# VectorE's order at the end of each head pair, the first step's order on ScalarE and GpSimd, and a third bank for the first products

## The chip, the cores and the metric

One core of one Trainium2 chip runs the whole program in one launch. The metric is the device time of that launch in microseconds, as a median of several runs. On a core, TensorE multiplies matrices, VectorE and ScalarE work on rows of vectors, GpSimd works on vectors and SyncE starts the DMAs. The program writes each engine's instructions in one list; an engine takes its list in order and waits on semaphores that the others count up.

## The reference

The input is layer-normalised, goes through lightning attention with a decay per head (16 heads of 128, blocks of 64 tokens in the reference, of 128 in the kernel), is RMS-normalised and gated, projected back, and multiplied by the SiLU of a router's mixture. Cut to what matters here:

```python
x = L0_attn_hidden_states                  # (4, 512, 512): 4 sequences of 512
xn = layernorm(x)
qkv = silu(xn @ w_qkv.T)                   # q, k, v of 16 heads
def step(kv, blk):
    o_inter = (q * q_decay) @ kv
    o_intra = ((q @ k.T) * diag_decay) @ v
    kv_new = block_decay * kv + (k * k_decay).T @ v
    return kv_new, o_inter + o_intra
out = norm_w * (out * rsqrt(mean(out * out) + eps))
s = (sigmoid(xn @ w_gate.T) * out) @ w_out.T
flat = xn.reshape(B * S, H)
scores = softmax(flat @ router_weight.T + router_bias)
topk_w, topk_idx = top_k(scores, 8)
g = silu(flat * sum(topk_w) + einsum(topk_w, expert_bias[topk_idx]))
return x + s * g
```

## The kernel before

The weights come in eight pairs of heads, the tokens in two halves (two sequences of 512 each). A half is a run over the eight pairs, so there are 16 steps, numbered `ss` 0 to 15; step 0 is the prologue, written out by hand, and `step(...)` on each engine writes steps 1 to 15. Step 8 (`close`) also finishes the output of the first half, step 15 (`final`) is the last; steps 6 and 14 carry the router's columns too.

Every matrix is split into a high and a low part in fp32r and a product is three matmuls. The products of queries and keys (groups `QK0` and `QK1`, one per head of the pair) and of the gates (`GATE`) go by seven block products (`p1`, `p2`, `p6`, `p5`, `p7`, `p4`, `p3` in this order) in place of eight; between them VectorE takes the partial sums out of the banks `st_ps` (`e1` to `e7`), ScalarE applies SiLU or tanh (`act_c11`, `act_c22`, `act_c21`, `act_c12`). Step 0 uses plain products (`direct_block(j)`, j 0 to 11), with the transposes of the tokens (`fill`) among them, banks `st_ps[0]` and `st_ps[1]` in turn.

A head h and a sequence b of a step make a unit (h, b), and for each there are, in this order: `turn_and_score` on TensorE (keys turned, scores into `score_ps`), `score_decay` on VectorE (scores times decay into `probs`, line 1561, which waits for the scores and for the head output two units before, since `probs` has one buffer per sequence), `query_decay` on VectorE (line 1568), `kv_products` on TensorE (line 591, into `tk_ps`), `states` on VectorE (lines 1577 and 1580), `head_output` on TensorE (lines 606 and 609), `gate_head` on VectorE (line 1589), `take_square` on ScalarE (line 1015) and `add_square` on GpSimd (line 1338). The gated heads are split into `gate_hi` (ScalarE, `gate_high`, line 1028) and `gate_lo` (VectorE, `gate_low`, line 1593) and go into `output_tile` (lines 616 to 618).

A transition is the end of a step's GATE group and the start of the next step's QK0. TensorE runs there p4, `head_output(ss, 0, 1)`, `kv_products(ss, 1, 0)`, p3, then p1 and p2 of the next QK0, `kv_products(ss, 1, 1)` and p6. The last `kv_products` waits for `states(ss, 1, 0)`, since both use `tk_ps`. p6 waits for the next QK0's `e1` (line 1517), which takes p1's sum out of `st_ps[0]`. VectorE runs e5, `score_decay(1, 1)`, `query_decay(1, 0)`, `gate_low(0, 0)`, `query_decay(1, 1)`, `states(1, 0)`, e7 (line 1552), then, after ScalarE's `act_c12` (line 986), `gate_head(0, 1)` and e1.

The weights land in one buffer `land_a`. ScalarE makes `w_hi` from it (`raw_hi` for the blocks as loaded, line 917; `sums_hi` for their sums, line 922), GpSimd makes `w_lo` (`raw_lo`, line 1289; `sums_lo`, line 1307) and the sums themselves in place (`weight_sums`, lines 1297 to 1303). The output weights go the same way (`out_hi`, lines 937 and 945; `out_lo`, line 1317). The prologue's spills of tokens to DRAM stand ahead of the load of group 4's weights in SyncE's queue.

Of the kernel before, what the change touches and what calls it, by code (L numbers as in the profile page):

```python
# [36 lines left out]
def lightning_block(nc: bass.Bass, x, wgrp, wv, wo, consts_d, router_w, expert_b, out):  # L37
# [6 lines left out]
    with ExitStack() as ctx:  # L44
# [134 lines left out]
        def group(ss, g):  # L179
            return 3 * ss + g  # L180
# [49 lines left out]

        def direct(j):

            row, b = j % 2, j % 4 // 2
            return ((R11, R12), (R21, R22))[row], ((B11, B21), (B12, B22))[b], places(j // 4)[2 * row + b]
# [176 lines left out]
        def _(pe):  # L411
            def fill(bp, f):
# [5 lines left out]
                if fill_bank(bp, f) is v_ps:  # L418
                    pe.wait_ge(v_taken, 4)
                if f // 2 in (T1, T3, T2, T4):  # L420
                    pe.wait_ge(t_row, 4 * bp + {T1: 1, T3: 2, T2: 3, T4: 4}[f // 2])
# [18 lines left out]
            def direct_block(j):  # L440

                wblks, xblks, _ = direct(j)
                n, buf, ps = j // 4, j // 4 % 2, st_ps[j % 2]
                if j >= 2:
                    pe.wait_ge(acted, j - 1)
# [27 lines left out]
            def p1(ss, g, buf):  # L473
                n = group(ss, g)
                pe.wait_ge(acted, 4 * (n - 1) + A_C21)
                pe.wait_ge(w_l, 2 * n + 1)
                if g == QK0:
                    tokens_there(ss, B11)
                block_product(st_ps[0], buf, A11, B11, True, False)

            def p2(ss, g, buf):
# [4 lines left out]
                if group(ss, g) == 3:  # L486
                    pe.wait_ge(acted, 12)
# [368 lines left out]
        def _(act):  # L856
# [42 lines left out]
            def act_direct(j):  # L899
# [8 lines left out]
                act.activation(direct(j)[2], st_ps[j % 2][:, :], func, scale=scale).then_inc(acted, 1)  # L908
# [135 lines left out]
            def step(bp, ss, odd):  # L1044
# [5 lines left out]
                raw_hi(group(ss, QK1), buf[1])  # L1050
                decays(ss, odd)
                act.preload_act_table(ACT.Silu)
                act_c11(ss, QK0)
                if ss == 1:
# [4 lines left out]
                take_square(before, 1, 0)  # L1059
                gate_high(before, 1, 0)  # L1060
                act_c22(ss, QK0)
                act_c21(ss, QK0)
                take_square(before, 1, 1)
                act_c12(ss, QK0)
                if ss == 1:
                    out_hi(0, 0)
# [176 lines left out]
        def _(pool):  # L1243
# [113 lines left out]
            def step(bp, ss, odd):  # L1357
# [5 lines left out]
                add_square(bp0, before, 0, 1)  # L1363
                raw_lo(group(ss, QK1), buf[1])
                mask_decay(ss)
                weight_sums(group(ss, QK1))
                add_square(bp0, before, 1, 0)
# [76 lines left out]
        def _(dve):  # L1444
# [247 lines left out]
            def step(bp, ss, odd, pair_next):  # L1692
# [94 lines left out]
                e5(ss, GATE)  # L1787
                score_decay(ss, 1, 1)
                if close:
                    sum0(7)  # L1790
                    scale0(6)
# [3 lines left out]
                query_decay(ss, 1, 0)  # L1795
                gate_low(ss, 0, 0)
                query_decay(ss, 1, 1)
                states(ss, odd, 1, 0)
# [146 lines left out]
```

## Time and profile before

| what | us |
|---|---|
| median of 3 runs | 1179.84 |
| lowest and highest | 1179.35, 1181.41 |
| the profiled execution: its own time | 1181.1 |
| the profiled execution: its span | 1179.3 |
| TensorE busy in it | 1104.1 (94%) |
| VectorE, ScalarE, GpSimd busy | 625.4, 508.3, 570.1 |

The span is from the first to the last instruction on the core. TensorE's matmuls overlap each other a little in the records, so its busy share is an upper bound of the work in it. The mean granted clock is 0.99 of full speed.

### The profile page before, as it was taken

The page shows a single profiled execution, that of the slowest core. Times are in us where ns is not written, and L with a number is a line of the kernel's source. Part 1 is how long each engine was busy: PE and PEld are TensorE (multiplying, and loading weights), DVE is VectorE, ACT ScalarE, POOL GpSimd, SP SyncE. Part 2 cuts the span into 40 slices and gives each one's busy share as a digit, 9 for nine tenths or more (in the row PEclk, how much of TensorE's full clock was granted, in tenths as well). Part 3 has the DMA queues.
Part 4 walks back from the last instruction along what each step waited for, and adds up shares of the span by engine and source line. Part 5 has one row for each costly group of instructions (what it writes and reads, how often), then busy time and mean ns, then how long its engine had stood idle before and what let it go on. Part 6 is the DMA issues. An engine that isn't in the chain of part 4 may idle for free.

```text
span 1179.3 us, 17081 instructions
## 1 busy us (share of the span) xinstructions
PE 1104.1 (94%) x6546; PEld 967.2 (82%) x6546; DVE 625.4 (53%) x1080; ACT 508.3 (43%) x813; POOL 570.1 (48%) x450
## 2 busy tenths in 40 slices
PE   5998999999999999999999899999999999999985
PEld 4987879798887979888797787988888798888874
DVE  6653454535545453566547545454454545455766
ACT  5644353443525344452553525334352533545242
POOL 4554454454446444453627636445453643526244
PEclk9998999999999999999999999999999999999998
DMA  6262111101111110112814111011111111010021
GB/s 238 85 242 67 36 36 48 43 19 54 36 37 36 54 37 19 36 55 72 303 37 143 42 49 36 21 53 35 37 42 48 36 32 53 25 36 19 36 72 72
DMA packets 28079, 73.10 MB, mean 62 GB/s; under 512 B 3040, under 2 KB 3168, under 8 KB 28000
## 3 DMA queue, kind: packets, MB, share of 16 engines
q1 hardware_dynamic: 28000, 72.02, 18.6%
q8 instruction: 53, 0.87, 0.3%
q14 instruction: 26, 0.21, 0.1%
HBM read 59.43 MB, written 12.58 MB: 61 GB/s over the span
## 4 chain that ended last, share of the span: by engine, by line
PE 84%; DVE 9%; ACT 3%; issue 3%; POOL 1%; DMA 1%; POOLq 0%; SPq 0%; DVEq 0%; ACTq 0%
PE st_ps L464 11%; PE st_ps L466 10%; PE st_ps L465 10%; PE head_ps L606 5%; PE score_ps L580 5%; PE out_ps L616 5%; PE v_ps L554 5%; PE v_ps L556 5%; PE v_ps L555 5%; PE out_ps L617 5%; PE out_ps L618 5%; DVE q_t L1568 4%; PE head_ps L609 3%; PE tk_ps L591 2%; PE tk_ps L572 2%
## 5 line engine op out<-in xcount | busy, mean ns | idle before, releaser
L464 PE MATMUL st_ps<-xt_hi,w_hi 128*128 128x512 f32 x630 | 260.2, 413 | 22.2 <-DVE q_t L1517 22.2
L466 PE MATMUL st_ps<-xt_hi,w_lo 128*128 128x512 f32 x630 | 248.4, 394 | 0.0
L465 PE MATMUL st_ps<-xt_lo,w_hi 128*128 128x512 f32 x630 | 247.3, 393 | 0.0
L1289 POOL TENSOR_TENSOR w_lo<-land_a,w_hi 128x768 fp32r<-128x768 f32 x45 | 82.8, 1839 | 238.6 <-ACT w_hi L917 238.6
L1602 DVE TENSOR_TENSOR acc<-acc,out_ps 128x512 f32<-128x512 f32 x120 | 82.4, 687 | 210.6 <-PE out_ps L618 210.4
L1307 POOL TENSOR_TENSOR w_lo<-land_a,w_hi 128x1024 fp32r<-128x1024 f32 x45 | 112.2, 2494 | 104.1 <-ACT w_hi L922 104.1
L464 PEld LDWEIGHTS st_ps<-xt_hi,w_hi 128*128 128x128 f32 x630 | 119.8, 190 | 45.4 <-DVE q_t L1517 24.9
L466 PEld LDWEIGHTS st_ps<-xt_hi,w_lo 128*128 128x128 f32 x630 | 119.1, 189 | 26.6
L465 PEld LDWEIGHTS st_ps<-xt_lo,w_hi 128*128 128x128 f32 x630 | 119.9, 190 | 20.8
L554 PE MATMUL v_ps<-wv_hi,xt_hi 128*128 128x256 f32 (+1 forms) x472 | 135.8, 288 | 0.0
L556 PE MATMUL v_ps<-wv_hi,xt_lo 128*128 128x256 f32 (+1 forms) x472 | 134.3, 285 | 0.0
L555 PE MATMUL v_ps<-wv_lo,xt_hi 128*128 128x256 f32 (+1 forms) x472 | 134.3, 284 | 0.0
L1338 POOL TENSOR_TENSOR acc_sq<-acc_sq,square 128x512 f32<-128x512 f32 x60 | 79.7, 1328 | 99.8 <-ACT square L1015 99.8
L1561 DVE TENSOR_TENSOR probs<-score_ps,decay 128x512 f32<-128x512 f32 x64 | 44.2, 691 | 110.2 <-PE score_ps L580 61.0
L999 ACT ACTIVATE v_row<-v_ps 128x512 f32<-128x512 f32 x55 | 32.9, 598 | 154.9 <-PE v_ps L556 154.9
L616 PE MATMUL out_ps<-wo_hi,gate_hi 128*128 128x512 f32 x242 | 96.4, 398 | 1.1 <-DVE acc L1602 1.0
L617 PE MATMUL out_ps<-wo_lo,gate_hi 128*128 128x512 f32 x242 | 94.7, 391 | 0.0
L618 PE MATMUL out_ps<-wo_hi,gate_lo 128*128 128x512 f32 x242 | 94.5, 390 | 0.0
L606 PE MATMUL head_ps<-probs,v_row 128*128 128x128 f32 x496 | 88.4, 281 | 6.2 <-ACT square L1015 6.2
L554 PEld LDWEIGHTS v_ps<-wv_hi,xt_hi 128*128 128x128 f32 x472 | 89.9, 191 | 1.8
L555 PEld LDWEIGHTS v_ps<-wv_lo,xt_hi 128*128 128x128 f32 x472 | 90.0, 191 | 1.8
L556 PEld LDWEIGHTS v_ps<-wv_hi,xt_lo 128*128 128x128 f32 x472 | 89.9, 190 | 0.0
(295 smaller groups left out, 2225.2 us busy)
## 6 DMA issues: line engine op xcount, KB each, us to landing
land_a<-wgrp_dram SPq DMA_DIRECT2D x48, 512.0 KB, 3.6
land_b<-wv_dram SPq DMA_DIRECT2D x16, 512.0 KB, 3.6
land_b<-wo_dram SPq DMA_DIRECT2D x16, 512.0 KB, 3.6
xt_hi<-spill_hi SPq DMA_DIRECT2D x16, 256.0 KB, 5.1
xt_lo<-spill_lo SPq DMA_DIRECT2D x16, 256.0 KB, 6.7
out_dram<-acc SPq DMA_DIRECT2D x16, 256.0 KB, 2.0
spill_hi<-gate_hi SPq DMA_DIRECT2D x11, 256.0 KB, 2.0
spill_lo<-gate_lo SPq DMA_DIRECT2D x11, 256.0 KB, 2.5
```

What stands on the lines that cost most here:

```text
L464: pe.matmul(ps[:, :], w_h2, x_h2, start=first and k == 0, stop=False, skip_group_check=True)
L465: pe.matmul(ps[:, :], w_h2, x_l2, start=False, stop=False, skip_group_check=True)
L466: end = pe.matmul(ps[:, :], w_l2, x_h2, start=False, stop=last and k == 1, skip_group_check=True)
L554: pe.matmul(dst, x_h2, w_h2, start=k == 0, stop=False, skip_group_check=True)
L555: pe.matmul(dst, x_h2, w_l2, start=False, stop=False, skip_group_check=True)
L556: end = pe.matmul(dst, x_l2, w_h2, start=False, stop=k == KC - 1, skip_group_check=True)
L606: last = pe.matmul(ps[:, at], v_row[:, b, c, h * HD:(h + 1) * HD], probs[:, b, c, :], start=True, stop=c == 0)
L616: pe.matmul(ps[:, :], hi[:, h, at], wo_hi[:, h, :], start=h == 0, stop=False)
L617: pe.matmul(ps[:, :], hi[:, h, at], wo_lo[:, h, :], start=False, stop=False)
L618: last = pe.matmul(ps[:, :], lo[:, h, at], wo_hi[:, h, :], start=False, stop=h == 1)
L1289: pool.tensor_tensor(flat(w_lo[:, buf, 0:3, :, :]), flat(land_a[:, 0:3, :, :]), flat(w_hi[:, buf, 0:3, :, :]).bitcast(F32), ALU.subtract). ...
L1307: pool.tensor_tensor(flat(w_lo[:, buf, 3:7, :, :]), flat(land_a[:, :, :, :]), flat(w_hi[:, buf, 3:7, :, :]).bitcast(F32), ALU.subtract).th ...
```

## The change

It does these things:

- **Every step, VectorE, in the transition.** `query_decay(1, 0)` and `gate_low(0, 0)` stand ahead of `score_decay(1, 1)`, and `states(1, 0)` stands ahead of `query_decay(1, 1)`. In step 8 `sum0(7)` stands ahead of them all, and in the last step `sum1(4)` and `sum1(5)` are now behind the first two.
- **Step 1, ScalarE.** `raw_hi` of QK1 (group 4) stands behind `act_c22`, no longer ahead of the decays; `out_hi(0, 0)` stands ahead of `act_c21`, no longer behind `act_c12`; `take_square(0, 1, 0)` stands ahead of `gate_high(0, 0, 0)` and its waits for the spills.
- **Step 1, GpSimd.** `mask_decay` and `add_square(0, 1, 0)` stand ahead of `raw_lo` of QK1.
- **Prologue, TensorE.** `direct_block(0)` to `(2)` use three banks, `st_ps[0]` to `st_ps[2]`; from j = 3 on the two banks alternate the other way round. Block 2 waits for no activation. `fill(1, 0)`, the next use of `st_ps[2]`, waits for the third activation. The wait of the first p1 is for 12 activations now, and the one ahead of p2 is gone.

```diff
+        def direct_bank(j):
+            return st_ps[j] if j < 3 else st_ps[(j + 1) % 2]
...
+                if (bp, f) == (1, 0):
+                    pe.wait_ge(acted, 3)
...
-                n, buf, ps = j // 4, j // 4 % 2, st_ps[j % 2]
-                if j >= 2:
-                    pe.wait_ge(acted, j - 1)
+                n, buf, ps = j // 4, j // 4 % 2, direct_bank(j)
+                if j >= 3:
+                    pe.wait_ge(acted, j - 2 if j < 5 else j - 1)
...
-                pe.wait_ge(acted, 4 * (n - 1) + A_C21)
+                pe.wait_ge(acted, 4 * n if n == 3 else 4 * (n - 1) + A_C21)
...
-                if group(ss, g) == 3:
-                    pe.wait_ge(acted, 12)
...
                 take_square(before, 0, 1)
-                raw_hi(group(ss, QK1), buf[1])
+                if ss > 1:
+                    raw_hi(group(ss, QK1), buf[1])
                 decays(ss, odd)
                 act.preload_act_table(ACT.Silu)
                 act_c11(ss, QK0)
+                take_square(before, 1, 0)
                 if ss == 1:
...
                     gate_high(0, 0, 0)
-                take_square(before, 1, 0)
                 gate_high(before, 1, 0)
                 act_c22(ss, QK0)
+                if ss == 1:
+                    raw_hi(group(ss, QK1), buf[1])
+                    out_hi(0, 0)
                 act_c21(ss, QK0)
                 take_square(before, 1, 1)
                 act_c12(ss, QK0)
-                if ss == 1:
-                    out_hi(0, 0)
...
                 add_square(bp0, before, 0, 1)
+                if ss == 1:
+                    mask_decay(ss)
+                    add_square(bp0, before, 1, 0)
                 raw_lo(group(ss, QK1), buf[1])
-                mask_decay(ss)
+                if ss > 1:
+                    mask_decay(ss)
                 weight_sums(group(ss, QK1))
-                add_square(bp0, before, 1, 0)
+                if ss > 1:
+                    add_square(bp0, before, 1, 0)
                 add_square(bp0, before, 1, 1)
...
                 e5(ss, GATE)
+                if close:
+                    sum0(7)
+                query_decay(ss, 1, 0)
+                gate_low(ss, 0, 0)
                 score_decay(ss, 1, 1)
                 if close:
-                    sum0(7)
                     scale0(6)
                 if final:
                     sum1(4)
                     sum1(5)
-                query_decay(ss, 1, 0)
-                gate_low(ss, 0, 0)
+                states(ss, odd, 1, 0)
                 query_decay(ss, 1, 1)
-                states(ss, odd, 1, 0)
```

VectorE at the end of step 2, before: e4 and e5 of the gates, the second scores, the two query decays with `gate_lo` between them, the states, e7, then `gate_head` and e1, e2 of step 3.

```order
L1540 COPY gated<-st_ps 128x512
L1546 TENSOR_TENSOR gated<-gated,st_ps 128x512
L1561 TENSOR_TENSOR probs<-score_ps,decay 128x512
L1568 TENSOR_TENSOR q_t<-q_t,decay 128x384
L1593 TENSOR_TENSOR gate_lo<-gated,gate_hi 128x512
L1568 TENSOR_TENSOR q_t<-q_t,decay 128x384
L1577 COPY state<-tk_ps 128x128
L1580 SCALAR_TENSOR_TENSOR state<-state,pair_cols,tk_ps 128x128 x2
L1552 TENSOR_TENSOR gated<-gated,st_ps 128x512
L1589 SCALAR_TENSOR_TENSOR gated<-gated,head_ps 128x512
L1517 COPY q_t<-st_ps 128x512
L1524 TENSOR_TENSOR q_t<-q_t,st_ps 128x512
```
The same place now (the same lines are ten higher in the changed file):

```order
L1550 COPY gated<-st_ps 128x512
L1556 TENSOR_TENSOR gated<-gated,st_ps 128x512
L1578 TENSOR_TENSOR q_t<-q_t,decay 128x384
L1603 TENSOR_TENSOR gate_lo<-gated,gate_hi 128x512
L1571 TENSOR_TENSOR probs<-score_ps,decay 128x512
L1587 COPY state<-tk_ps 128x128
L1590 SCALAR_TENSOR_TENSOR state<-state,pair_cols,tk_ps 128x128 x2
L1578 TENSOR_TENSOR q_t<-q_t,decay 128x384
L1562 TENSOR_TENSOR gated<-gated,st_ps 128x512
L1599 SCALAR_TENSOR_TENSOR gated<-gated,head_ps 128x512
L1527 COPY q_t<-st_ps 128x512
L1534 TENSOR_TENSOR q_t<-q_t,st_ps 128x512
```
The first query decay and `gate_lo` moved ahead of `probs`, and the states ahead of the second query decay; e7 and all behind it stand where they stood.

ScalarE in step 1, before, from `raw_hi` to `act_c22`:

```order
L917 ACTIVATE w_hi<-land_a 128x768 [waits made,w_in]
L954 ACT_TABLE_LOAD [waits q_decayed,probs_set]
L954 ACTIVATE decay<-consts,pair_cols 128x128 [waits cols_set]
L955 ACTIVATE decay<-consts,pair_cols 128x128
L954 ACTIVATE decay<-consts,pair_cols 128x128
L955 ACTIVATE decay<-consts,pair_cols 128x128
L1052 ACT_TABLE_LOAD
L965 ACTIVATE q_t<-q_t 128x512 [waits joined]
L1028 ACTIVATE gate_hi<-gated 128x512 [waits spilled2,gated_set,spilled1,spilled0]
L1015 ACTIVATE square<-head_ps 128x512 [waits sq_added,gated_set]
L1028 ACTIVATE gate_hi<-gated 128x512 [waits gated_set]
L971 ACTIVATE k_t<-k_t 128x512 [waits joined]
```
The same engine now, from the last exponential to `act_c21`:

```order
L958 ACTIVATE decay<-consts,pair_cols 128x128
L1056 ACT_TABLE_LOAD
L968 ACTIVATE q_t<-q_t 128x512 [waits joined]
L1018 ACTIVATE square<-head_ps 128x512 [waits sq_added,gated_set]
L1031 ACTIVATE gate_hi<-gated 128x512 [waits spilled2,gated_set,spilled1,spilled0]
L1031 ACTIVATE gate_hi<-gated 128x512 [waits gated_set]
L974 ACTIVATE k_t<-k_t 128x512 [waits joined]
L920 ACTIVATE w_hi<-land_a 128x768 [waits made,w_in]
L940 ACTIVATE land_b<-land_b,pair_cols 128x512 [waits cols_set,wo_in]
L940 ACTIVATE land_b<-land_b,pair_cols 128x512
L948 ACTIVATE wo_hi<-land_b 128x1024 [waits xt_turned,t_row,wo_scaled]
L983 ACTIVATE k_t<-st_ps 128x512 [waits scored,prod]
```
`w_hi` (`raw_hi`) moved from ahead of the table load to behind `act_c22`, the square ahead of the wait for the spills, and the three of `out_hi` ahead of `act_c21`.

TensorE in the prologue, the end of `v_fill(0, 0, 0)` and the start of `direct_block(2)`, before, with bank numbers:

```order
L555 MATMUL v_ps<-wv_lo,xt_hi 128x256
L556 MATMUL v_ps<-wv_hi,xt_lo 128x256
L454 MATMUL st_ps0<-xt_hi,w_hi 128x512 [waits xt_l,acted]
L455 MATMUL st_ps0<-xt_lo,w_hi 128x512
L456 MATMUL st_ps0<-xt_hi,w_lo 128x512
```
And now:

```order
L558 MATMUL v_ps<-wv_lo,xt_hi 128x256
L559 MATMUL v_ps<-wv_hi,xt_lo 128x256
L459 MATMUL st_ps2<-xt_hi,w_hi 128x512 [waits xt_l]
L460 MATMUL st_ps2<-xt_lo,w_hi 128x512
L461 MATMUL st_ps2<-xt_hi,w_lo 128x512
```
The bank is the third one and the wait for `acted` is gone.

## Rows read from the trace of the kernel before

**Rows 1.** The page, section 1: busy time, share of the span, instructions

```profile
PE 1104.1 (94%) x6546; PEld 967.2 (82%) x6546; DVE 625.4 (53%) x1080; ACT 508.3 (43%) x813; POOL 570.1 (48%) x450
```

**Rows 2.** Waits of PE: line, releaser: us in total, times, longest us

```profile
PE st_ps L464 <- DVE q_t L1517: 22.2, 13, 1.7
...
PE tk_ps L591 <- issue: 13.7, 15, 2.2
...
PE head_ps L606 <- ACT square L1015: 6.2, 3, 3.6
...
PE st_ps L454 <- ACT q_t L908: 1.0, 1, 1.0
```

**Rows 3.** Timeline of VectorE, 352 to 383: start us, us, what [idle before]

```profile
363.54 0.69 DVE L1561 TENSOR_TENSOR probs<-score_ps,decay 128x512 f32<-128x512 f32 x1 [2.86 <-PE head_ps L609]
...
365.22 2.75 DVE L1568 TENSOR_TENSOR q_t<-q_t,decay 128x384 f32<-128x384 f32 x1
...
368.20 0.73 DVE L1580 SCALAR_TENSOR_TENSOR state<-state,pair_cols,tk_ps 128x128 f32<-128x128 f32 x2
...
368.85 0.68 DVE L1552 TENSOR_TENSOR gated<-gated,st_ps 128x512 f32<-128x512 f32 x1
...
370.91 0.68 DVE L1517 COPY q_t<-st_ps 128x512 f32<-128x512 f32 x1
```

**Rows 4.** Timeline of GpSimd, the same stretch

```profile
364.86 2.69 POOL L1317 TENSOR_TENSOR wo_lo<-land_b,wo_hi 128x1024 fp32r<-128x1024 f32 x1 [5.25 <-ACT wo_hi L945]
```

**Rows 5.** Timeline of TensorE, 356 to 376

```profile
369.04 0.91 PE L591 MATMUL tk_ps<-v_row,k_row 128*128 128x128 f32 x6 [0.87 <-issue]
...
371.65 0.50 PE L464 MATMUL st_ps<-xt_hi,w_hi 128*128 128x512 f32 x1 [1.71 <-DVE q_t L1517]
```

**Rows 6.** Lines 1568 and 1580: duration ns min/median/max, first and last start

```profile
L1568 DVE TENSOR_TENSOR q_t<-q_t,decay x64: 545/548/2762, 44.7 to 1144.0; 128x384 f32<-128x384 f32 x64
...
L1580 DVE SCALAR_TENSOR_TENSOR state<-state,pair_cols,tk_ps x128: 346/348/351, 61.1 to 1149.1; 128x128 f32<-128x128 f32 x128
```

**Rows 7.** Windows: us; PE, PEld, DVE, ACT, POOL busy; granted clock, DMA, GB/s

```profile
98.50:104.30 5.80, 5.80 (x21) 5.23 (x22) 1.59 (x3) 0.88 (x2) 2.95 (x3) 0.51 0.00 1
...
158.60:228.40 69.80, 67.23 (x395) 59.10 (x395) 33.37 (x56) 28.46 (x44) 32.61 (x27) 0.98 0.13 38
...
228.40:296.80 68.40, 65.83 (x396) 57.73 (x395) 34.60 (x57) 28.45 (x44) 32.73 (x27) 1.00 0.13 39
```

**Rows 8.** Timeline of ScalarE in the first step

```profile
91.95 0.85 ACT L917 ACTIVATE w_hi<-land_a 128x768 fp32r<-128x768 f32 x1 [4.74 <-DMA land_a<-wgrp_dram]
...
92.82 1.28 ACT L954 ACT_TABLE_LOAD   x1
...
107.00 1.32 ACT L937 ACTIVATE land_b<-land_b,pair_cols 128x512 f32<-128x512 f32 x2
...
108.35 1.06 ACT L945 ACTIVATE wo_hi<-land_b 128x1024 fp32r<-128x1024 f32 x1
```

**Rows 9.** Timeline of GpSimd in the first step

```profile
92.88 1.84 POOL L1289 TENSOR_TENSOR w_lo<-land_a,w_hi 128x768 fp32r<-128x768 f32 x1 [3.49 <-ACT w_hi L917]
...
97.10 0.72 POOL L1299 TENSOR_TENSOR land_a<-land_a 128x256 f32<-128x256 f32 x1
...
109.49 2.35 POOL L1317 TENSOR_TENSOR wo_lo<-land_b,wo_hi 128x1024 fp32r<-128x1024 f32 x1 [2.69 <-ACT wo_hi L945]
```

**Rows 10.** Timeline of TensorE in the first step

```profile
98.48 1.20 PE L606 MATMUL head_ps<-probs,v_row 128*128 128x128 f32 x4 [3.63 <-ACT square L1015]
...
112.14 0.47 PE L616 MATMUL out_ps<-wo_hi,gate_hi 128*128 128x512 f32 x1
```

**Rows 11.** Timelines of TensorE and VectorE at the end of step 8

```profile
650.43 1.65 PE L591 MATMUL tk_ps<-v_row,k_row 128*128 128x128 f32 x6 [2.76 <-ACT k_row L1007]
...
657.03 0.68 DVE L1517 COPY q_t<-st_ps 128x512 f32<-128x512 f32 x1
```

**Rows 12.** Timeline of ScalarE at the end of the last step

```profile
1146.40 0.72 ACT L1036 ACTIVATE tail_row<-tail_row,ffn_small 128x512 f32<-128x512 f32 x1 [0.97 <-DVE tail_row L1660]
```

More of the change, by code:

```diff
@@ L907, in act_direct @@
                     act.wait_ge(xt_turned, filled(1, 3))
-                act.activation(direct(j)[2], st_ps[j % 2][:, :], func, scale=scale).then_inc(acted, 1)
+                act.activation(direct(j)[2], direct_bank(j)[:, :], func, scale=scale).then_inc(acted, 1)
             def raw_hi(n, buf):
```

## The prediction

> **What bounds the kernel now.** I read the page first: TensorE is busy 94% of the span [rows 1], so only its idle time and its slow clock can be won. Then its waits [rows 2]: nearly all the idle time in the body is one pattern, 13 waits of 1.7 us for e1 and, just before each, 0.87 us ahead of the last `kv_products` (13 of the 15 "issue" waits). The timelines of one transition (step 4 to 5) tell why. VectorE waits 2.86 us for `head_output(0, 1)`, runs the scores at 363.54, then `query_decay(1, 0)`, `gate_low`, then `query_decay(1, 1)` at 365.22 for 2.75 us, the states, e7 at 368.85, and e1 at 370.91 [rows 3]. TensorE gets its `kv_products` at 369.04, when the states are done, and p6 at 371.65, when e1 is [rows 5]. So from 363.54 on the chain is VectorE's, with one ScalarE activation between e7 and `gate_head`.
>
> The odd row is the decay of 2.75 us: the same instruction takes 0.55 as a rule, and up to 2.76 [rows 6]. GpSimd's `out_lo` has 364.86 to 367.55 [rows 4], and the decay ends 0.42 us behind that. Its two inputs both lie in SBUF, as both inputs of `out_lo` do. The states instruction has one input in `tk_ps`, and all 128 of them took 0.35 us [rows 6], whatever GpSimd did.
>
> **The 13 ordinary transitions.** `query_decay(1, 0)` (0.55) and `gate_low` (0.6) go into the wait of 2.86 us, with 1.7 us to spare; nothing queued behind them is needed sooner. Taken alone this would let `query_decay(1, 1)` start at 364.2, before GpSimd. But the states go ahead of it: scores 363.54 to 364.15, states (0.3 and two of 0.35) to 365.2. `out_lo` waits only for ScalarE, so it starts at 364.86 as before, and the decay, next at 365.2, meets it again. What is won is smaller, and I take it in two parts. First, before, `gate_low` held `out_lo` back from 364.86 to 365.30: its 2.69 us are 2.35 where nothing does [rows 9], so it ends at 367.2, not 367.55. Second, the states no longer stand behind the decay. The decay ends at 367.2 + 0.42 = 367.6, and e7 starts there and not at 368.85 [rows 3]: 1.3 us earlier, and all behind it by as much, e1 and p6 too (p6 at 370.35). The 0.87 us ahead of `kv_products` go as well, but they lie inside the same chain and are not counted: TensorE waits longer for e1 instead, about 1.5 us in one piece. 13 x 1.3 = **16.9 us**.
>
> The Trainium skill (SBUF — State Buffer, "Who interferes with whom") says that a VectorE instruction with two SBUF inputs and a GpSimd instruction that reads SBUF lock each other out, the first to start keeping the port to its end. It speaks against this order of states and decay, and the 2.75 us row agrees; were it false, the decay would take 0.55 and the transition would gain about 2.6 us instead of 1.3, which is the rival on the better side below.
>
> **Slow clock.** Two of the 13 transitions (into steps 2 and 9) are followed by a stretch at half clock, 1.2 in place of 2.4 GHz. A step with one lasts 69.8 us and the next without 68.4 [rows 7], so 1.4 us each. Ahead of them TensorE had stood idle 0.87 and 1.71 us, as at all 13; now it stands 1.5. Single waits of 1.0 to 1.7 us elsewhere had no such stretch behind them. I take both as gone: **2.8 us**, between 0 and 2.8, and further stretches as a rival.
>
> **Prologue.** The wait of 1.0 us for the first activation [rows 2] goes, since block 2 has a bank of its own; the next one on that bank is `fill(1, 0)`, far later. The transposed tokens that it needs as well are split by then. TensorE has no other wait until step 1, so all of it comes through: **1.0 us**.
>
> **Step 1.** ScalarE stood 4.74 us waiting for group 4's weights until 91.95, then two table loads of 1.28 and the decays followed [rows 8], and `head_output(0, 1, 1)` came 3.63 us late, at 98.48 [rows 10], for the square behind them. Then TensorE ran at a mean clock of 0.51 from 98.5 to 104.3 [rows 7], a loss of some 2.8 us, and a wait of 1.2 for `k_row` followed. Now (in the trace's times, the prologue's 1.0 left out) the decays and loads begin at 87.1 and end at 91.0, the square is made at 92.9 to 93.4, as soon as the gated head is, and TensorE goes on at 94.85 without a wait. It reaches p3's end at 94.85 + 1.35 + 2.8 = 99.0. Here a new wait is late: `turn_and_score` needs `act_c21`, and ahead of it ScalarE now has `act_c22` (at 96.3, when e5 is done), `raw_hi` (0.85), and `out_hi` (1.32 + 1.06) [rows 8]: 96.3 + 0.6 + 0.85 + 2.4 = 100.1, and c21 to 100.75. That is a wait of 1.7 us. Then scores to 102.0, values (2.9) to 104.9, the second scores to 106.1. The first `output_tile` needs `out_lo`. GpSimd: `raw_lo` from 97.8 (1.84), four sums of 0.81 start to start (0.72 each), a square of 1.3, `out_lo` 2.35 [rows 9]: 97.8 + 1.9 + 3.2 + 1.3 + 2.4 = 106.6, with 0.3 for a meeting with VectorE's decay 106.9. So the tile starts at 106.9 and not at 112.14 [rows 10]: **5.2 us**. At the worst another half-clock stretch costs 1.4 to 2.8 of them; at the best the two small waits are missing (+0.8). The load of the next weights waits for `sums_lo`, 2.4 us behind `out_lo` as before, and moves along with all this.
>
> **Step 8.** Before, ScalarE's `silu0(7)` stood waiting for `sum0(7)` behind the scores, with the k rows queued behind it, and `kv_products` came 2.76 us late [rows 11]. Now `sum0(7)` runs in VectorE's wait, and `kv_products` and p3 follow `head_output` at 647.7. VectorE: scores 647.8, `scale0(6)` 0.66, states 1.0, then the decay behind GpSimd's add that `scale0(6)` lets go (1.3 us from 649.2), so to 650.9; e7 0.65, activation and hand-over 0.8, `gate_head` 0.6, `scale0(7)` 0.65, e1 at 653.55 in place of 657.03 [rows 11]. GpSimd's add and square, for which TensorE waits next, hang on `scale0(7)` and come as much earlier: **3.5 us**.
>
> **Last step.** `act_c12` stands behind `silu1(6)`, which waited 0.97 us for its sum [rows 12]. The sum is now behind the scores, two sums, the states and one decay, all done by 1144.4, so that wait goes: **1.0 us**.
>
> Sum: 16.9 + 2.8 + 1.0 + 5.2 + 3.5 + 1.0 = 30.4 us. The profiled execution took 1181.1 us with a span of 1179.3, the median is 1179.84, 1.3 below that execution; the terms are differences within the span and I take them off the median: **1149.4 us**.
>
> **Rivals.**
> - *Half clock after more transitions.* 1.5 us of idle time in one piece stands against 0.87 + 1.71 in two. If four transitions have a stretch behind them, 2 x 1.4 more than before and 2.8 not won: 1155. If all 13 have one, 11 x 1.4 = 15.4 more and 2.8 not won: 1167.6. Against it: 11 of 13 with more idle time had none. Chance 0.09, most of it at the short end.
> - *The states wait for GpSimd too,* because they come while it holds the port. Then states 367.2 to 368.2, decay to 368.75, e7 0.1 earlier than before, and 13 x 0.1 = 1.3 in place of 16.9: 1165. The 128 rows of equal length [rows 6] speak against it. Chance 0.03.
> - *The decay is not caught*: it starts before `out_lo` takes the port, or overlaps it. It ends at 365.7, e7 follows at once, e1 at 367.8, before `kv_products` is through, and TensorE waits for nothing: the 2.6 us of [rows 5] go each time, 33.5 in place of 16.9, 1133. ScalarE would have to hand over 0.35 us later than it did. Chance 0.05.
> - *Slower.* The half-clock stretch of step 1 lasted 5.8 us and cost 2.8 [rows 7]. If the new single wait brought such a one after each of the 15 transitions, 15 x 2.8 = 42 us would stand against 27.6 won, 1194. It decides from 1.84 us of cost per transition. In the trace that length came only after 3.6 us of idle time. Chance 0.02.
> - *Nothing in the body*, since the chain through e7 were hidden: there is no wait of TensorE that would take its place, so I give it 0.01, at about 1168.
>
> **How the numbers follow.** The forecast has 0.78, and 0.02 go to what none of this sees, 0.015 of it within the bound and 0.005 slower. Its own range: 13 x 0.2 us either way on the transition, 0 to 2.8 for the clock, and 2 either way on steps 1 and 8: 1145.5 to 1154. The range goes to 1156, to take in the rival with four stretches; left out are 0.05 below and about 0.10 above, and some 0.05 of the forecast's own ends. Faster by over 0.2% (2.4 us, about what a measurement of this kernel can tell from no change) is 0.96, within it 0.015, slower 0.025.
>
> **What would show it.** In the profile after: the waits of TensorE for e1 still 13, of about 1.5 us, and no 0.87 ahead of `kv_products`; the second decay of a transition still 2.3 us or so long, behind an `out_lo` of 2.35; no wait at `head_output` of step 1 but one of 1.7 us at its first `turn_and_score`; ordinary steps of 67.1 us in place of 68.4. I am wrong if steps stay at 68.4, if the decay is 0.55 us long, or if the granted clock falls behind many transitions.

## The result, and the profile after

The changed kernel takes 1150.77 us (median of 4 runs, 1149.68 to 1152.22) against 1180.48 for the kernel before in the same comparison. The ratio is 0.975, 95% interval 0.9733 to 0.9766: 29.7 us or 2.5% less. 1149.4 was forecast. The profiled execution took 1152.22 us with a span of 1150.4; its span is 28.9 us below that of before.

The page of the changed kernel (its lines are some three to eleven higher than before; the second row is busy us with the share of the span, the third the granted clock in tenths by slice):

```profile
span 1150.4 us, 17081 instructions
...
PE 1094.5 (95%) x6546; PEld 962.5 (84%) x6546; DVE 628.1 (55%) x1080; ACT 508.2 (44%) x813; POOL 568.2 (49%) x450
...
PEclk9999999999999999999999999999999999999997
```
TensorE is busy 95% in place of 94% [rows 1], with 9.6 us less of busy time. Most of this is slow clock that is gone: its trace has 6.8 us in stretches at half clock between start and end where the kernel before has 17.1, and full clock comes 13.3 us after the start in place of 18.8. Half of these two differences is 7.9 us. Its waits:

```profile
PE st_ps L469 <- DVE q_t L1527: 21.3, 14, 1.5
...
PE head_ps L609 <- ACT square L1018: 2.6, 2, 1.4
...
PE st_ps L609 <- DVE state L1590: 2.3, 1, 2.3
...
PE tk_ps L575 <- ACT k_t L983: 1.4, 1, 1.4
...
PE out_ps L619 <- POOL wo_lo L1322: 0.8, 1, 0.8
...
PE tk_ps L594 <- issue: 0.3, 1, 0.3
```
The 13 waits of 1.7 us for e1 [rows 2] are 14 of 1.5 (the fourteenth is at step 8), the pieces of 0.87 ahead of the `kv_products` are gone (0.3 is left, in step 1), and so are the 3.6 us at the head output of step 1, the 2.8 for the k row at step 8 and the 1.0 at block 2. New are 1.4 us for `act_c21` and 0.8 for `out_lo`, both in step 1, and 2.3 for the states in the last step where it was 1.0. One transition, step 4 to 5, on VectorE, GpSimd and TensorE, in this order:

```profile
347.96 0.55 DVE L1578 TENSOR_TENSOR q_t<-q_t,decay 128x384 f32<-128x384 f32 x1
...
348.43 0.68 DVE L1603 TENSOR_TENSOR gate_lo<-gated,gate_hi 128x512 fp32r<-128x512 f32 x1
...
350.91 0.69 DVE L1571 TENSOR_TENSOR probs<-score_ps,decay 128x512 f32<-128x512 f32 x1 [1.79 <-PE head_ps L612]
...
351.83 0.73 DVE L1590 SCALAR_TENSOR_TENSOR state<-state,pair_cols,tk_ps 128x128 f32<-128x128 f32 x2
...
352.48 2.56 DVE L1578 TENSOR_TENSOR q_t<-q_t,decay 128x384 f32<-128x384 f32 x1
...
354.96 0.68 DVE L1562 TENSOR_TENSOR gated<-gated,st_ps 128x512 f32<-128x512 f32 x1
...
357.02 0.68 DVE L1527 COPY q_t<-st_ps 128x512 f32<-128x512 f32 x1
```

```profile
352.23 2.39 POOL L1322 TENSOR_TENSOR wo_lo<-land_b,wo_hi 128x1024 fp32r<-128x1024 f32 x1 [5.25 <-ACT wo_hi L948]
```

```profile
355.38 0.83 PE L594 MATMUL tk_ps<-v_row,k_row 128*128 128x128 f32 x6
...
357.75 0.50 PE L469 MATMUL st_ps<-xt_hi,w_hi 128*128 128x512 f32 x1 [1.55 <-DVE q_t L1527]
```
The first decay and `gate_lo` stand in the wait, which is 1.79 us now instead of 2.86 [rows 3]. The states run beside `out_lo` at their usual 0.73 for two. The second decay asks at 352.48, 0.25 us after `out_lo` has started, and takes 2.56; `out_lo` itself is 2.39 us and not 2.69 [rows 4]. The windows (us; PE, PEld, DVE, ACT, POOL busy; granted clock, DMA, GB/s) of step 2 to 3, of a stretch in the last step, and of the stretch of step 1 that had 0.51 before:

```profile
151.10:218.20 67.10, 65.55 (x395) 57.74 (x394) 33.23 (x56) 28.36 (x44) 32.95 (x27) 1.00 0.14 40
...
1119.40:1126.20 6.80, 5.75 (x17) 4.59 (x17) 4.99 (x7) 4.24 (x6) 3.21 (x3) 0.51 0.01 2
...
98.50:104.30 5.80, 5.50 (x46) 5.31 (x46) 1.50 (x3) 3.52 (x6) 5.64 (x5) 1.00 0.00 1
```
The step lasts 67.1 us at full clock in place of 69.8 and 68.4 [rows 7]. The stretch at half clock is now at the end.

Read from start of e1 to start of e1 in the timelines of VectorE, so that the terms can be set side by side (us):

| stretch | before | after | difference | forecast |
|---|---|---|---|---|
| start to the first e1 | 88.06 | 85.94 | 2.1 | 1.0 |
| step 1 | 76.21 | 69.72 | 6.5 | 5.2 + 1.3 |
| steps 3 to 5, 11 to 13 | 68.4 | 67.1 | 1.28 each | 1.3 each |
| steps 6, 7, 9, 14 (with the router or other work besides) | 71.32, 69.28, 71.30, 71.35 | 70.07, 67.99, 70.03, 70.02 | 1.25 to 1.33 | 1.3 each |
| steps 2 and 10 | 69.85, 69.71 | 67.13, 67.15 | 2.7, 2.6 | 1.3 + 1.4 each |
| step 8 | 77.14 | 73.71 | 3.4 | 3.5 |
| last e1 to the end of the span | 104.7 | 105.9 | -1.2 | 1.0 |

The rows add up to 29 us, the difference of the spans. The stretch at 729 us, which the prediction gives to step 9, is at the start of step 10 by this count; its price and number are as told there.

### The profile page after: what moved, and what is told of

Same layout as the page of the kernel before. It is cut to its first block, busy times and chain, and to the rows that moved or that the text cites. A ratio compares the mean times of both kernels' runs of the same rounds, so it can differ in the third digit from the quotient of the medians.

```text
span 1150.4 us, 17081 instructions
## 1 busy us (share of the span) xinstructions
PE 1094.5 (95%) x6546; PEld 962.5 (84%) x6546; DVE 628.1 (55%) x1080; ACT 508.2 (44%) x813; POOL 568.2 (49%) x450
## 4 chain that ended last, share of the span: by engine, by line
PE 85%; DVE 8%; issue 2%; ACT 2%; POOL 2%; DMA 0%; POOLq 0%; SPq 0%; DVEq 0%; ACTq 0%
PE st_ps L469 11%; PE st_ps L471 11%; PE st_ps L470 11%; PE v_ps L557 5%; PE v_ps L559 5%; PE out_ps L619 5%; PE v_ps L558 5%; PE out_ps L620 5%; PE out_ps L621 5%; PE head_ps L609 5%; PE score_ps L583 5%; PE head_ps L612 3%; DVE q_t L1578 3%; PE tk_ps L594 2%; PE tk_ps L575 2%
## 5 line engine op out<-in xcount | busy, mean ns | idle before, releaser
L1343 POOL TENSOR_TENSOR acc_sq<-acc_sq,square 128x512 f32<-128x512 f32 x60 | 82.4, 1374 | 79.9 <-ACT square L1018 79.9
```

## The experiments

Their traces are compared by the same intervals. Times are medians (for two kernels a single run); the kernel before, timed beside each group of them on the same chip, took 1180.0 to 1181.1 us.

**The second decay ahead of the states** (on the changed kernel):

```diff
-                states(ss, odd, 1, 0)
                 query_decay(ss, 1, 1)
+                states(ss, odd, 1, 0)
```

> The changed kernel with the second query decay and the states of each transition in the other order: scores, second decay, states. Theory (GpSimd's out_lo and the decay lock each other out, the first to start goes first): the decay starts at 364.2 in the old trace's times and ends at 364.75, out_lo asks at 364.86, so the decay takes 0.55 us, e7 follows the states at about 365.8, e1 is done at about 368.5, before TensorE is through its kv_products at 368.85. TensorE's 13 waits of 1.55 us for e1 go, steps of 67.1 us become 65.6, the time is 1150.8 - 13 x 1.55 = 1130.6 us. First rival (the decay takes long because it reads what ScalarE and VectorE have just written, or by its place behind the scores, and GpSimd is not the cause): it takes 2.5 us again, the states come behind it, and the time is 13 x 1.0 us longer, 1164. Second rival (only the order against the wait counts, 1.15 us of work moved into it): the time stays at 1150.8.

Measured: 1126.44 us (1124.29 to 1127.58), ratio 0.9543, 0.9529 to 0.9557. VectorE in a transition, and then GpSimd's `out_lo` of it:

```profile
344.55 0.69 DVE L1571 TENSOR_TENSOR probs<-score_ps,decay 128x512 f32<-128x512 f32 x1 [1.79 <-PE head_ps L612]
...
345.15 0.55 DVE L1578 TENSOR_TENSOR q_t<-q_t,decay 128x384 f32<-128x384 f32 x1
...
345.94 0.73 DVE L1590 SCALAR_TENSOR_TENSOR state<-state,pair_cols,tk_ps 128x128 f32<-128x128 f32 x2
...
346.58 0.68 DVE L1562 TENSOR_TENSOR gated<-gated,st_ps 128x512 f32<-128x512 f32 x1
...
348.65 0.68 DVE L1527 COPY q_t<-st_ps 128x512 f32<-128x512 f32 x1
...
345.87 2.41 POOL L1322 TENSOR_TENSOR wo_lo<-land_b,wo_hi 128x1024 fp32r<-128x1024 f32 x1 [5.25 <-ACT wo_hi L948]
```

```profile
L1578 DVE TENSOR_TENSOR q_t<-q_t,decay x64: 547/549/2787, 41.9 to 1085.7; 128x384 f32<-128x384 f32 x64
```
The decay asks at 345.15, 0.72 us before `out_lo`, and takes 0.55. So do the second decays of all 13 ordinary transitions, each of which takes 2.56 in the changed kernel (and 2.75 in the kernel before). The last row is over all 64 decays: its median is 0.55 in every kernel here, and its longest, 2.79, is one in step 1. The instruction, its operands and its place right behind the scores are those that a rival for the length would have blamed. e7 starts 2.0 us behind the scores in place of 4.0, and TensorE's waits for e1 are gone but one. Steps last 65.2 us, 1.92 less than 67.12 where 1.55 was recorded as idle, so the time came 4 us lower than expected: a wait of TensorE costs about 0.37 us more here than its record says. Why it does was not tested.

**`out_lo` in two halves** (on the changed kernel):

```diff
-                pool.tensor_tensor(wo_lo[:, :, :].rearrange("p a f -> p (a f)"), land_b[:, :],
-                                   wo_hi[:, :, :].rearrange("p a f -> p (a f)").bitcast(F32),
-                                   ALU.subtract).then_inc(wo_l, 1)
+                for h in range(2):
+                    last = pool.tensor_tensor(wo_lo[:, h, :], land_b[:, h * HID:(h + 1) * HID],
+                                              wo_hi[:, h, :].bitcast(F32), ALU.subtract)
+                last.then_inc(wo_l, 1)
```

> The changed kernel with GpSimd's out_lo as two instructions of 512 columns in place of one of 1024. Theory (the port is held for one instruction, and goes to who waits when that ends): the second query decay, which asks at 365.2, starts when the first half is done at about 366.15 and ends at 366.6, e7 comes 1.0 us earlier and TensorE's 13 waits for e1 are 0.5 us in place of 1.55: 1137. The decay is 1.4 us long in place of 2.56. Rival (GpSimd keeps the port over both, or the decay waits for the whole job): 1151 and the decay 2.5 us or more.

Measured: one run, 1137.63 us. GpSimd's two halves in one row, then VectorE's decay and e7:

```profile
350.13 2.86 POOL L1323 TENSOR_TENSOR wo_lo<-land_b,wo_hi 128x512 fp32r<-128x512 f32 x2 [5.25 <-ACT wo_hi L948]
...
350.37 1.46 DVE L1579 TENSOR_TENSOR q_t<-q_t,decay 128x384 f32<-128x384 f32 x1
...
351.75 0.68 DVE L1563 TENSOR_TENSOR gated<-gated,st_ps 128x512 f32<-128x512 f32 x1
```
The decay takes 1.46 us (1.46 or 1.47 in all 13 transitions): it gets in between the halves, which together take 2.86 where one instruction took 2.39, 0.47 more, about one decay. Steps last 66.05 us, 1.07 less than the changed kernel's. So what makes the decay long is the one GpSimd instruction that is under way when it asks, whatever work GpSimd still has. The two runs together show the cause: the order alone makes 0.55 or 2.56 of it, and halving the other side's instruction makes 1.46.

**Only the states ahead of the second decay** (on the kernel before), run once, and then timed as the same kernel:

```diff
-                query_decay(ss, 1, 1)
                 states(ss, odd, 1, 0)
+                query_decay(ss, 1, 1)
```

> The kernel before with only the states of each transition put ahead of the second query decay; the first decay and gate_low stay behind the second scores. Theory: states from 365.3 to 366.3 in the old trace's times beside out_lo, the decay is caught until 367.55 and ends at 367.97, e7 follows there and not at 368.85: 0.9 us earlier 13 times, 11.4 us, and 0 to 2.8 of half-clock stretches: 1166 to 1169. Rival (the states wait for GpSimd as the decay does): no change, and line 1580 shows rows of over 1 us. TensorE's wait for e1 becomes 1.7 us in one piece, none ahead of the kv_products.

> The kernel with only the states ahead of the second decay again, now timed. In its first look the steps without a half-clock stretch were 0.92 us shorter each, as expected, but 7 of the 13 ordinary transitions had such a stretch (2 in the kernel before), after a wait of TensorE of 1.85 us in one piece. Theory (that is a trait of this kernel and not of that execution): mean granted clock about 0.981 in most runs and a median within 3 us of the kernel before. Rival (the look was unlucky): clock 0.99 and 1167 to 1170.

Measured: 1180.43 in the single run; timed 1178.34 (10 runs, 1173.88 to 1184.48), ratio 0.9991, 0.997 to 1.0012. The states beside `out_lo`, the decay and e7, and TensorE's wait in another transition:

```profile
364.63 0.73 DVE L1580 SCALAR_TENSOR_TENSOR state<-state,pair_cols,tk_ps 128x128 f32<-128x128 f32 x2
...
365.27 1.78 DVE L1568 TENSOR_TENSOR q_t<-q_t,decay 128x384 f32<-128x384 f32 x1
...
366.98 0.67 DVE L1552 TENSOR_TENSOR gated<-gated,st_ps 128x512 f32<-128x512 f32 x1
...
300.85 0.50 PE L464 MATMUL st_ps<-xt_hi,w_hi 128*128 128x512 f32 x1 [1.84 <-DVE q_t L1517]
```
In the ordinary transitions the mechanism did what was expected: the two states take 0.73 us, the decay 1.78, and e7 starts 4.35 us behind the scores (362.63) in place of 5.31. Of two neighbouring steps one is at full clock and one is not:

```profile
226.90:294.30 67.40, 65.55 (x395) 57.71 (x394) 32.40 (x56) 28.32 (x45) 33.28 (x26) 1.00 0.12 40
...
294.30:363.20 68.90, 67.06 (x395) 59.22 (x394) 32.46 (x56) 28.49 (x45) 32.73 (x26) 0.98 0.12 39
```
67.4 us without a stretch at half clock, 0.95 less than 68.4, and 68.9 with one. In the single run 7 of the 13 ordinary transitions had such a stretch, in the profiled run of the timed ones 10, where the kernel before had 2. At 1.45 us each the further 5 and 8 stretches take back 7.3 of the 12.4 us (13 x 0.95) in the one and 11.6 in the other. The rest is lost in the last step. There the new order puts the decay behind `out_lo`, which it was ahead of before, and TensorE's wait for the states becomes 3.4 us where it was 1.0:

```profile
1140.07 2.69 DVE L1568 TENSOR_TENSOR q_t<-q_t,decay 128x384 f32<-128x384 f32 x1
...
PE st_ps L606 <- DVE state L1580: 3.4, 1, 3.4
```
e7 comes 2.0 us later by this, and a stretch of 6.8 us at half clock follows, as in the changed kernel. From the last e1 to the end it takes 110.4 and 110.3 us in the two traces, 104.7 before: 4.2 us more besides one ordinary stretch. Together that makes 0.9 us less and 3.4 more than before; the spans have 0.7 less and 3.4 more. The mean granted clock of the ten timed runs lies between 0.975 and 0.984; it was 0.990 in ten of the 13 runs of the kernel before beside them. The expectation of 1166 to 1169 for the single run was wrong by both losses. What was expected of the timed runs held: the low clock is a trait of the kernel and not of one execution.

**Only VectorE's part of the change** (all of the diff's last piece, nothing else):

```diff
 e5(ss, GATE)
+query_decay(ss, 1, 0)
+gate_low(ss, 0, 0)
 score_decay(ss, 1, 1)
-query_decay(ss, 1, 0)
-gate_low(ss, 0, 0)
-query_decay(ss, 1, 1)
 states(ss, odd, 1, 0)
+query_decay(ss, 1, 1)
```

> The kernel before with only VectorE's part of the change. Theory (each part works in its own place and they add up): 16.9 us on 13 transitions, 2.8 of half-clock stretches that stay away, 3.5 in step 8 and 1.0 in the last step, 24.2 us less than before: 1156. Rival (step 1 and the prologue carry more than their terms, because the first bubble also sets how the rest lies): 1158 to 1165. TensorE's waits for e1 are 1.55 us, 13 times, and no 0.87 us ahead of the kv_products; the wait of 3.6 us in step 1 is still there.

Measured: 1155.67 us (1155.42 to 1156.04), ratio 0.9793, 0.9778 to 0.9807. Two of TensorE's waits, and a window in step 1:

```profile
PE st_ps L464 <- DVE q_t L1517: 21.3, 14, 1.6
...
PE head_ps L606 <- ACT square L1015: 6.1, 3, 3.5
```

```profile
98.00:104.00 6.00, 6.00 (x42) 5.45 (x42) 2.80 (x5) 2.69 (x5) 3.44 (x3) 1.00 0.00 1
```
Steps last 67.1 us and step 8 73.75. The wait of 3.5 us in step 1 is still there (the 6.1 are its and two of 1.3 in step 8), yet the window behind it is at full clock: step 1 lasts 72.21, which is 4.0 less than before where the transition gives 1.3. Six traces here have this order of step 1 and its wait of 3.5 to 3.8 us. The half clock follows it in four (the kernel before, the bank-only kernel and both of the states-only kernel) and not in two (this one and the pair-only kernel below). In those four full clock had come 18.7 to 21.5 us after the start of the program, in the two at 13.3 and 13.5. Whether that or the kernel decides was not tested.

**Only step 1** on ScalarE and GpSimd, and **only the third bank**, each on the kernel before:

```diff
 act_c11; take_square(0, 1, 0); gate_high x2; act_c22
+raw_hi; out_hi(0, 0)
 act_c21; ...
```

> The kernel before with only the first step's order on ScalarE and GpSimd changed. Theory: 5.2 us less than before, 1175; the wait of 3.6 us ahead of the head output goes, one of 1.4 us for act_c21 and one of 0.8 us for out_lo come, and no half-clock stretch there. Rival (the clock falls all the same behind the new waits): 1178. The transitions keep their 0.87 and 1.71 us.

```diff
-n, buf, ps = j // 4, j // 4 % 2, st_ps[j % 2]
+n, buf, ps = j // 4, j // 4 % 2, direct_bank(j)
```

> The kernel before with only the third bank in the prologue. Theory: TensorE's wait of 1.0 us at block 2 goes and all of it comes through, 1179.2. Rival (the other trace reached step 1 2.1 us earlier, so the bank is worth 2.1): 1178. Second rival (hidden further on, in step 1, where the weights' load sets the time): no change. In the profile the start of the first kv_products of step 1 tells the first two apart, read beside where the clock became full at the start.

Measured: 1174.48 us (5 runs, 1172.25 to 1178.4), ratio 0.9956, 0.9938 to 0.9973, for step 1; 1180.10 us (10 runs, 1176.97 to 1182.46), ratio 0.9997, 0.9986 to 1.0009, for the bank. In the first the wait of 3.6 us in step 1 is gone, 1.4 for `act_c21` and 0.8 for `out_lo` have come, and step 1 has no half clock; it lasts 71.01 us, 5.2 less than before. Of these 2.7 are the half clock and 2.5 the order, as the vector-only kernel tells (72.21 with neither, less 67.13 for its own transitions, is 5.1; 71.01 less 68.39 is 2.6). The profiled run of this kernel is the slowest of its five, with half clock behind 4 of the 13 ordinary transitions. The bank brings block 2 nearer to the values ahead of it by 1.2 us (2.95 in place of 4.15 from start to start) and the first `kv_products` of step 1 nearer by 1.3, and the time does not show it. The granted clock does: 0.984 to 0.988 in eight of its ten runs, where the kernel before had 0.990 in all but one of 14, and its trace has half-clock stretches into steps 2 and 3, one of them twice as long (steps of 71.16 and 69.80). With its 1.2 us all transitions lie 1.2 us earlier, and the stretches fall otherwise. I did not make a run that shifts the transitions alone, so that this is what eats the gain is likely and not shown.

**Only the first decay and `gate_lo` moved** (on the kernel before; the states stay last):

```diff
 e5(ss, GATE)
+query_decay(ss, 1, 0)
+gate_low(ss, 0, 0)
 score_decay(ss, 1, 1)
-query_decay(ss, 1, 0)
-gate_low(ss, 0, 0)
 query_decay(ss, 1, 1)
 states(ss, odd, 1, 0)
```

> The kernel before with only the first query decay and gate_low moved ahead of the second scores in each transition (with the sums of step 8 and the last step as in the change); the states stay behind the second decay. Theory (the gain of VectorE's part is the pair's; the states ahead of the decay, which came with it, give most of it back, since they push the decay into out_lo): what the decay-first kernel has below the changed one, 24.3 us, comes off the 1155.7 of VectorE's part alone: 1131 us. Rival (the two orders differ only together with step 1 and the bank, through where the waits fall): 1140 or more. No wait of TensorE for e1 in the ordinary transitions, all second decays 0.55 us.

Measured: 1132.78 us (1128.19 to 1134.95), ratio 0.961, 0.958 to 0.9639. Steps of 65.2 us, second decays of 0.55 us and no waits for e1 in the ordinary transitions. This is 23 us below VectorE's whole part: the states ahead of the decay are a loss, once the pair is in the wait. Its runs differ by the clock, 0.997 in the one of 1128.2 and 0.991 in the three of 1130.9 to 1135.0.

**Step 8 as before, and the last step as before** (VectorE's order there alone, on the changed kernel):

```diff
+if close:                      # or: if final
+    score_decay(ss, 1, 1); sum0(7); scale0(6)
+    query_decay(ss, 1, 0); gate_low(ss, 0, 0)
+    query_decay(ss, 1, 1); states(ss, odd, 1, 0)
+else:
     ...
```

> The changed kernel with VectorE's order in the transition of step 8 alone as before (sum0(7) and scale0(6) behind the scores, then the rest). Theory: the wait of 2.8 us for the k row is back and all behind it comes 3.5 us later: 1154.2. Rival (the square and the table loads behind it set the time there whatever VectorE does): 1151.

> The changed kernel with VectorE's order in the last step alone as before. Theory of the prediction: 1.0 us more, 1151.8. Rival (in the last step the change moved act_c12 forward by 1.0 but its longer wait of TensorE for the states, 2.3 us, brings a half-clock stretch that takes it back): no change or up to 1 us less, and no stretch of 6.8 us near the end in its profile.

Measured: 1151.94 us (1151.52 to 1153.44) for step 8, 1151.63 (1150.18 to 1151.79) for the last step, against 1150.77 of the changed kernel in another session. TensorE's `kv_products` of step 8 with its wait is back:

```profile
631.60 0.94 PE L594 MATMUL tk_ps<-v_row,k_row 128*128 128x128 f32 x6 [2.76 <-ACT k_row L1010]
```
Step 8 lasts 76.16 us against 73.71: its order is worth 2.45 us. The kernel before had 77.14 there, the other 1.0 being the half clock behind that wait, which this kernel has not. The median for step 8 shows only 1.2, and the rest lies where the clock falls: the span here is 1149.8 with full clock from early on and none of the half clock in the last step before the end. From the last e1 to the end it takes 103.95, the changed kernel's profiled execution 105.9, and both run the same code there. So the last step's new order is worth 104.7 - 103.95 = 0.75 us, and a stretch of 6.8 us at half clock took 1.95 in the profiled execution. With the last step as before the same piece takes 104.8, as in the kernel before, though a stretch of 3.4 us at half clock lies in it. It costs nothing that can be seen there; TensorE's wait of 0.99 us for a state is gone with it and the wait behind is 1.03 in place of 1.41. The median for the last step is 0.9 us above the changed kernel's, and could not by itself tell 0.75 or 1.0 from nothing, since each kernel's four runs lie 1.6 to 2.5 us apart.

**Two versions further.** Step 1 once more, on the decay-first kernel, and on top of that the last step's `act_c12`:

```diff
 act_c11(ss, QK0)
+if ss == 1:
+    raw_hi(group(ss, QK1), buf[1])
 take_square(before, 1, 0)
 ...
-if ss == 1:
-    raw_hi(group(ss, QK1), buf[1])
-    out_hi(0, 0)
 act_c21(ss, QK0)
+if ss == 1:
+    out_hi(0, 0)
...
 out_hi(ss, odd)
+act_c12(ss, GATE)              # the second version only
 if final:
     silu1(5)
     silu1(6)
-act_c12(ss, GATE)
```

> The kernel with the second decay ahead of the states, and step 1 in another order: raw_hi of group 4 right behind act_c11, out_hi behind act_c21, and on GpSimd raw_lo ahead of the square. Theory: the weights have landed at 91.95 in the old trace's times, so raw_hi fits ahead of the square at 92.9; act_c21 is at 98.2, right behind p4, and out_lo is made by 102; the two waits of step 1, 1.4 and 0.8 us, go: 2.2 us less than the kernel with the decay first, 1128.4 if that has 1130.6. Rival (the k rows behind the sums, or the square behind raw_lo on GpSimd, become the late ones): no gain, a wait of 1 us or more at head_output or at the second turn_and_score in step 1.

> The kernel with the second decay first and step 1 in the other order (1124.4 us), and in the last step act_c12 on ScalarE ahead of silu1(5) and silu1(6). Theory: act_c12 stands 1.3 us behind two SiLUs that nobody waits for sooner, e7 is done when out_hi is, so gate_head and all behind it come 1.2 us earlier: 1123.1. Rival (GpSimd's weigh(5) and weigh(6) behind those SiLUs, or the clock at the end, set the time): 1124.4.

Measured: 1124.36 us (1122.7 to 1124.66), ratio 0.9514, 0.9496 to 0.9531, and 1124.58 (1122.88 to 1126.62), ratio 0.9528, 0.9505 to 0.9552. The first is the fastest kernel here, 2.1 us below the decay-first one by the medians, 1.7 by step 1 (66.07 against 67.76): the wait for `act_c21` is gone, 0.5 us for `out_lo` stay. The second brings nothing. TensorE's waits near the end, in the first and in the second:

```profile
PE st_ps L609 <- DVE state L1592: 2.1, 1, 2.1
...
PE v_ps L619 <- issue: 1.2, 1, 1.2
```

```profile
PE v_ps L619 <- issue: 3.1, 1, 3.1
...
PE st_ps L609 <- DVE state L1592: 1.0, 1, 1.0
```
The wait for the states fell from 2.1 to 1.0 us and the next one rose from 1.2 to 3.1: the gates' split for the output came no sooner. What sets it is GpSimd's addition of the square, as the rival had it in part. GpSimd takes `out_lo`, an addition for the tail and this one in turn, and gets to it 73.95 us behind the last e1 where it was 73.93 without the move; the addition then takes 1.72 us in place of 1.26. ScalarE's next square, with the gates' split behind it, waits for that:

```profile
1094.09 0.60 ACT L1018 ACTIVATE square<-st_ps 128x512 f32<-128x512 f32 x1 [2.59 <-POOL acc_sq L1344]
```
Without the move this wait was 1.29 us.

## Why the prediction was right

**The transition** (13 x 1.3) was right in size and in cause. The intervals give 1.28. Its two parts are there: `out_lo` at 2.39 in place of 2.69 and the decay's end 0.42 us behind it, and the states out from behind the decay. The states-only kernel gives 0.95, and the pair's move the other 0.33 on top of it. By itself the pair's move gives 3.2 (the pair-only kernel). The rival "the decay is not caught" was priced at 33.5 us against before; the decay-first kernel, which makes it true, has 3.2 x 13 = 41.6. The price was the sum of the recorded waits, 0.87 + 1.71 = 2.58, and a wait costs more than its record.

**The slow clock in the body** (2.8) was right in size: steps 2 and 10 (the second is the prediction's step 9) gave 1.4 and 1.3 besides. Its reason was thin. The forecast took it from waits of 1.0 to 1.7 us elsewhere that had no stretch behind them, and left out the one of 2.76 us at step 8, which had one. That single waits of 1.55 us would stay without was in part luck. The experiments put numbers to it: behind single waits of 1.55 us, none in the 13 ordinary transitions of the changed kernel, and none in those of the vector-only, step-8 and last-step ones; behind single waits of 1.85 us, 7 and 10 of 13 in two executions of the states-only kernel; behind 0.87 and 1.71 us, 2, 4 and 2 of 13 in the kernel before, the step-1-only and the bank-only one. Between the two kernels lie 0.3 us of wait, which is just what the pair's move gave. Each kernel's count is from one trace, and the length of the wait alone does not decide, as the wait of 3.5 us in step 1 shows. The rival of more stretches had 0.09, which was rather low: with only the states moved it is what happens, and most of the gain goes.

**The prologue** (1.0): the bank is worth 1.2 to 1.3 us in its place, a little more than the wait of 1.03. The other 0.8 of the 2.1 us lie ahead of it, at the start of the program, where full clock came 5.5 us earlier in the profiled execution of after. They are luck: the change has nothing there.

**Step 1** (5.2) came out at 5.2, with the two waits that it named, 1.38 and 0.80 us for 1.7 and 0.8. Half of it is a half-clock stretch that the old order has in four of its six traces, so by the order alone the term is 2.5.

**Step 8** (3.5) was 3.4, of which 2.45 are the order and 1.0 the clock. The prediction's working names only the order: it set new times at full clock against old ones with a half-clock stretch among them, and so took in the 1.0 without saying it.

**The last step** (1.0) came out worst: the order gave 0.75, and the profiled execution lost 1.95 to a half-clock stretch behind TensorE's wait of 2.3 us for the states. The step took `act_c12` forward and did not ask what TensorE does with the time; it waits there for the same chain in one piece of 2.34 us where it had 2.19 and 0.99. In the profiled execution it is -1.2 where 1.0 was forecast, more than the whole 1.5 us by which the spans' difference (28.9) stays below the sum (30.4); the prologue gave 1.1 of it back. The three other runs of the changed kernel had a mean clock of 0.997, as the step-8 kernel, whose trace has no stretch before the end, so they probably lost nothing there; the profiled one had 0.994.

## What to carry to other kernels

When an instruction has two lengths in a trace, look at what GpSimd is doing when it asks, and put it ahead of GpSimd's start rather than into the gap: here 0.7 us of order were worth 24 us. A move that lets an instruction come earlier can push another one into a collision; cost each order with the start times of the other engine beside it, and do so for every step that the edit touches: the same swap won 0.95 us in an ordinary transition of the kernel before and lost 2.0 in its last step. A shorter wait is not always worth its length: in this kernel whether TensorE's clock halves behind it decided over the same number of microseconds as the wait itself.

## What the runs showed of the hardware

- A VectorE instruction with both inputs in SBUF took 0.55 us alone and 2.56 when it asked 0.25 us after a GpSimd instruction with SBUF inputs had started, 1.46 when that instruction was half as long. The states instructions, with one input in PSUM, took 0.35 us in all 128 cases. The Trainium skill (SBUF — State Buffer, "Who interferes with whom") says that a VectorE instruction with two SBUF inputs contends with a GpSimd instruction that reads SBUF, and one with at most one SBUF input does not. The lengths here agree with it.
- A wait of TensorE cost more than its idle record: 1.55 us recorded, 1.92 won when it went (the decay-first kernel); 1.03 recorded, 1.2 won (bank-only); 2.58 in two waits, 3.2 won (pair-only).
- Behind single waits of 1.85 us the granted clock fell to half, 1.2 GHz, in 17 of 26 transitions, behind 1.55 us in none of 52 (four kernels). A stretch cost 1.4 us. The length of the wait does not decide alone: behind waits of 1.85 us the clock fell in some transitions of one trace and not in others, and behind the wait of 3.5 to 3.8 us in step 1 it fell in four traces of six. What else decides is open.
- The kernel before ran at a mean clock of 0.990 in most runs and of 0.994 in three of the 13 in one session, and those three took 1175.4 to 1175.5 us where the ten others took 1179.6 to 1182.9: the same program, 5 us apart by the clock alone.
